# A two-layer graph attention: one program instead of six blocks, no global centre, first units on a quarter of the adjacency, layer 1 prepared in layer 0's last chunk

## The reference

```
# layer 0: 4 heads of width 32
Wh = (x @ W).reshape(N, 4, 32)
e  = leaky_relu(s_src[:, None, :] + s_dst[None, :, :], 0.2)      # s = <Wh, a>
att = softmax(where(adj > 0, e, -9e15), axis=1)
x  = layernorm(x + elu(att @ Wh))
# layer 1: one head of width 128, in a hyperbolic space
t  = logmap0(x)
e  = leaky_relu(t @ a[:128] + (t @ a[128:]).T, 0.2)
att = softmax(where(adj > 0, e, -9e15), axis=1)
out = layernorm(x + proj(expmap0(att @ t)))
```

## Time and profile before

| | us |
|---|---|
| median of 3 runs | 1024.91 (1024.4 to 1026.4) |
| the profiled execution | 1024.66 |
| its span, first to last instruction | 1022.8 |
| TensorE, VectorE, ScalarE busy in it | 867.5, 853.7, 584.0 |
| GpSimd busy | 55.9 |
| mean granted clock of TensorE | 0.932 of full speed |
| moved by DMA | 68.84 MB, 67 GB/s over the span |

### The profile page before, as it was taken

The page is one execution under the profiler, slowest core; times in us unless marked ns, Lnnn a source line. Parts: engine busy times, 40 slices in busy tenths (PEclk is TensorE's granted clock), DMA queues, the critical chain, the costliest instruction groups (busy, mean ns, idle before and its releaser), DMA issues. The chain is left out here.

```text
span 1022.8 us, 25271 instructions
## 1 busy us (share of the span) xinstructions
PE 867.5 (85%) x10996; PEld 712.4 (70%) x10996; DVE 853.7 (83%) x1576; ACT 584.0 (57%) x640; POOL 55.9 (5%) x59
## 2 busy tenths in 40 slices
PE   6714999998999989998899704598999999999990
PEld 5614999998999989998899704354555555555550
DVE  5797788899998999889999678989878878788716
ACT  2478889996999869998768114361332514315101
POOL 1231000000000000000000005200000000000000
PEclk9756999999999999999999956799999999999996
DMA  8937756632666327031000023002032020320000
GB/s 146 166 66 195 96 65 72 81 162 43 74 74 123 127 24 85 23 130 79 23 3 3 1 85 104 1 1 93 11 104 77 27 92 10 103 76 27 0 10 12
DMA packets 30187, 68.84 MB, mean 67 GB/s; under 512 B 1346, under 2 KB 22276, under 8 KB 29444
## 3 DMA queue, kind: packets, MB, share of 16 engines
q0 software_dynamic: 4608, 16.78, 17.1%
q1 hardware_dynamic: 23300, 48.47, 13.3%
q10 hardware_dynamic: 2176, 2.10, 0.6%
HBM read 96.54 MB, written 21.14 MB: 115 GB/s over the span
## 5 line engine op out<-in xcount | busy, mean ns | idle before, releaser
L857 PE MATMUL bank<-moving,ring 128*128 128x99 bf16 (+1 forms) x6400 | 453.4, 219 | 11.6 <-DVE ring L817 11.6
L857 PEld LDWEIGHTS bank<-moving,ring 128*128 128x128 fp8e4 x6400 | 386.3, 97 | 14.2 <-DVE ring L817 13.9
L773 ACT ACTIVATE ring<-s_rows,scores 128x1024 fp8e4<-128x1024 f32 x352 | 373.1, 1140 | 28.7 <-PE bank L857 19.0
L1317 PE MATMUL bank<-moving,pair 128*128 128x387 bf16 x1792 | 300.1, 329 | 3.4 <-DVE evac L1406 3.4
L1317 PEld LDWEIGHTS bank<-moving,pair 128*128 128x128 fp8e4 x1792 | 175.8, 98 | 127.8 <-DVE evac L1406 3.8
L857 PE MATMUL bank<-moving,masks 128*128 128x99 bf16 x1792 | 237.8, 208 | 30.2 <-DVE ring L807 20.6
L857 PEld LDWEIGHTS bank<-moving,masks 128*128 128x128 fp8e4 x1792 | 174.4, 98 | 32.0 <-DVE ring L807 20.8
L1243 ACT ACTIVATE small<-small 128x4 f32<-128x4 f32 x24 | 4.9, 206 | 219.3 <-DVE small L1189 180.5
L807 DVE SCALAR_TENSOR_TENSOR ring<-ring,masks 128x1024 int32<-128x1024 int32 x88 | 107.3, 1220 | 15.3 <-ACT ring L773 15.1
L788 DVE TENSOR_SCALAR ring<-s_rows,neg_d 128x1024 uint8<-128x1024 f32 x160 | 109.6, 750 | 1.7 <-PEq L910 1.6
L817 DVE TENSOR_TENSOR ring<-masks,ring 128x1024 int32<-128x1024 int32 x72 | 88.2, 1225 | 17.1 <-PE bank L857 15.0
(11 more groups left out here) (217 smaller groups left out, 581.1 us busy)
## 6 DMA issues: line engine op xcount, KB each, us to landing
adj_tiles<-in_adj_dram POOLq DMA_DIRECT2D x32, 512.0 KB, 8.3
masks_kept<-masks SPq DMA_DIRECT2D x4, 4096.0 KB, 14.8
pair<-masks_kept SPq DMA_DIRECT2D x8, 2048.0 KB, 8.7
s_rows<-score_rows SPq DMA_DIRECT2D x16, 512.0 KB, 3.9
feat<-in_x_dram SPq DMA_DIRECT2D x4, 512.0 KB, 5.5
values_kept<-masks SPq DMA_DIRECT2D x1, 2048.0 KB, 15.6
s_rows<-score_rows SPq DMA_DIRECT2D x8, 256.0 KB, 8.5
out_dram<-result ACTq DMA_DIRECT2D x8, 256.0 KB, 2.1
```

The source lines that it names most:

```text
L773: last = act.activation(j_tile(below, k), s_rows[:, h % 2, :], ACT.Sign, bias=scores[:, j, h:h + 1], saturate=False)
L857: last = pe.matmul(bank[b][:, at + lo:at + hi], mask, moving[:, j, h, lo:hi], start=first, stop=(j == T - 1), skip_group_check=True)
L1317: last = pe.matmul(bank[2 * t + side][:, 0:PARTS * K1], j_tile1(pair[:, y, side, :], j)[:, t * P:(t + 1) * P], moving1[:, j, side * PARTS ...
```

## The change

All of both layers' fast path is one block; general attention is a second block behind it. Its parts:

- `bounds` and `exponents` are gone, with the extrema, the centre, the mean of the values and the treatment of rows without neighbours. Exponentials are taken straight from the scores by ScalarE; the row factor is one `lift` in layer 0. One flag is raised late in layer 1 (`raise_flag`) from the scores' extrema, the variances, empty rows, and a check of the adjacency: 64 parts of 2048 integers per partition, each loaded by POOL (1 MB) into one of two buffers and put through a Square with accumulation on ScalarE (`check_part`), two or three behind each group of signs of runs 2 to 7.
- The adjacency of chunk 0 comes in four quarters of columns (`load_quarter`, `turn_quarter`, `take_quarter`), and a unit waits only for its quarter. Head 0's weights are split before the units, those of heads 1 to 3 beside units 0 to 6. The score rows of heads 0 and 1 come from four matmuls of 512 columns instead of through HBM.
- `DIRECT` marks 12 of 32 units; the transposes for chunk 1 begin at unit 12.
- `take_head` and `take_run` lose the steps for empty rows, and `finish_ask` its minimum.
- In the last chunk, VectorE and ScalarE do root, logarithm, gains and exponentials of the first three chunks' rows and the weights of group 0; the last chunk's rows follow in run 0, before group 3.
- All eight signs of a group of run 0 are ScalarE's; POOL splits no weights.
- Results are stored by SP, not by ScalarE. The product of the residual with the inverse deviation moves under the tanh. Runs are unrolled.

```diff
-    DIRECT = [how == "D" for how in H // 2 * ("DD-D----" "DD-D-D--")]
+    DIRECT = [how == "D" for how in H * "DD-D----"]
+    CHECKS = 64
+    CHECK = N * N // P // CHECKS
...
+        def load_quarter(pool, k):
+            for q in range(NB):
+                pool.dma_start(quarter[:, k % 2, :].rearrange("p (q r n) -> p q r n", r=2, n=C)[:, q, :, :],
+                               adj_blocks[:, q, :, k * C:(k + 1) * C]).then_inc(quarter_in[k % 2], 16)
...
+        def check_part(act, k):
+
+            act.wait_ge(check_loaded[k % 2], 16 * (k // 2 + 1))
+            if k >= 2:
+                act.wait_ge(check_done, k - 1)
+            act.activation(check_out[k % 2], check_in[k % 2], ACT.Square, bias=minus_one[:, 0:1], scale=2.0,
+                           accum_out=checks[:, k:k + 1], saturate=False).then_inc(check_done, 1)
...
+                pool.wait_ge(unit_done, NC * U)
+                for k in range(CHECKS):
+                    if k >= 2:
+                        pool.wait_ge(check_done, k - 1)
+                    pool.dma_start(check_in[k % 2], adj_flat[:, k * CHECK:(k + 1) * CHECK]).then_inc(check_loaded[k % 2], 16)
...
+                take_quarter(act, 0)
+                round_part(act, 0, 1)
+
+                for c in range(NC):
+                    for u in range(U):
+                        act_unit(act, c, u)
...
+                        if c == 0:
+                            if u in (1, 3, 5):
+                                round_part(act, u // 2 + 1, 0)
+                            if u in (2, 4, 6):
+                                round_part(act, u // 2, 1)
+                                if u == 4:
+                                    act.wait_ge(scores_out, 16)
+                                take_quarter(act, u // 2)
...
+                for e in range(NR):
+                    fast_closing.act(act, e)
+                    for g in range(NG):
+                        if e + 2 < NR:
+                            signs(act, e + 2, g)
+                        while done < min(CHECKS, CHECKS * (e * NG + g + 1) // (NG * (NR - 2))):
+                            check_part(act, done)
+                            done += 1
...
+                        if c == 0:
+                            if u in (0, 2, 4):
+                                weigh_values(dve, u // 2 + 1)
+                                take_high(dve, u // 2 + 1)
+                            if u in (1, 3, 5):
+                                take_middle(dve, u // 2 + 1)
...
+                        if c == NC - 1:
+                            if u == 15:
+                                roots_ask(step, rows, 0, EARLY, roots_asked)
+                            if u == 17:
+                                dve.wait_ge(roots_given, 1)
+                                logs_ask(step, rows, inv_std, 0, EARLY, logs_asked)
+                            if u == 19:
+                                dve.wait_ge(logs_given, 1)
+                                gains(step, rows, inv_std, 0, EARLY, d1, s1, scores1_ready)
+                            if u == 22:
+                                late_weights(0)
+                            if u == 23:
+                                dve.wait_ge(kept, 16 * (NC - 1))
+                                dve.wait_ge(unit_done, (NC - 1) * U)
+                                weigh_group(dve, 0)
...
+                for e in range(NR):
+                    take_run(step, e)
+                    if e + 2 < NR:
                         for g in range(NG):
+                            split_group(dve, e + 2, g)
+                    if e == NR - 2:
+                        raise_flag(step)
```

More of the change, by code:

```diff
@@ new lines, in wait_s, with act_unit @@
+        def wait_s(engine, c, u):
+            h = u // UH
+            if c == 0 and h < 2:
+                engine.wait_ge(s_first, 2 * (h + 1))
+            else:
+                engine.wait_ge(s_in[h % 2], c * 32 + 16 * (h // 2))
+        def act_unit(act, c, u):
+            h, g = divmod(u, UH)
+            if g == 0:
+                wait_s(act, c, u)
+            if not ON_ACT[u]:
+                return
+            wait_slot(act, c, u)
+            below = below_slot(c, u)
+            for k in range(JU):
+                last = act.activation(j_tile(below, k), s_rows[:, h % 2, :], ACT.Sign,
+                                      bias=scores[:, g * JU + k, h:h + 1], saturate=False)
+            last.then_inc(signs_ready, 1)
+            if g == UH - 1:
+                act.wait_ge(signs_ready, c * NA + act_count(u + 1))
+                act.sem_inc(s_read_act, 1)
@@ new lines, in pe_unit @@
+        def pe_unit(pe, c, u):
+            h, g = divmod(u, UH)
+            if c == 0 and g == 0:
+                pe.wait_ge(side_done, 2 * (h + 1))
+            pe.wait_ge(unit_ready, c * U + (u + 1))
+            below = below_slot(c, u)
+            for t in range(CT):
+                b, at = t // 2, (t % 2) * W0
+                if g == 0 and t % 2 == 0 and (c > 0 or h > 0):
+                    pe.wait_ge(acc_taken, c * (H * NB) + ((h - 1) * NB + b + 1))
+                for k in range(JU):
+                    j = g * JU + k
+                    mine = slice(t * P, (t + 1) * P)
+                    of_below = j_tile(below, k)[:, mine]
+                    if DIRECT[u]:
+                        of_all = j_tile(masks[:, c % 2, :], j)[:, mine]
+                        weighed = ((of_all, 0, PARTS * K0), (of_below, 0, W0))
+                    else:
+                        weighed = ((j_tile(above_slot(c, u), k)[:, mine], 0, PARTS * K0), (of_below, PARTS * K0, W0))
+                    for mask, lo, hi in weighed:
+                        first = j == 0 and t % 2 == 0 and mask is weighed[0][0]
+                        last = pe.matmul(bank[b][:, at + lo:at + hi], mask, moving[:, j, h, lo:hi],
+                                         start=first, stop=(j == T - 1), skip_group_check=True)
+                if g == UH - 1 and t % 2 == 1:
+                    last.then_inc(acc_ready, 1)
+                elif t == CT - 1:
+                    last.then_inc(unit_done, 1)
+            if g == UH - 1:
+                pe.wait_ge(acc_ready, c * (H * NB) + (h + 1) * NB)
+                pe.sem_inc(unit_done, 1)
@@ new lines, in _ @@
+                split_group(dve, 0, 0)
+                take_head(step, NC - 1, H - 1)
+                dve.wait_ge(unit_done, NC * U)
+                weigh_group(dve, 1)
+                take_high1(dve, 1)
+                take_middle1(dve, 1)
+                split_group(dve, 0, 1)
+                close_piece(NC - 1, 0)
+                weigh_group(dve, 2)
+                take_high1(dve, 2)
+                take_middle1(dve, 2)
+                split_group(dve, 0, 2)
+                for n in range(1, 5):
+                    close_piece(NC - 1, n)
@@ new lines, in two_layer_gat, with flagged @@
+        general0 = General(0, H, D, lambda it, h: one(scores[:, bass.ds(it, 1), H + h:H + h + 1]))
+        general1 = General(1, 1, F, lambda it, h: g_s1[:, bass.ds(it, 1)])
+        general_closing = Closing("g_close", work=g_work1, result=g_result, small=g_small, stats=g_stats,
+                                  mean_var=g_mean_var[:, 0:RT, :], inv_std=g_inv_std)
+        def flagged(engine):
+            return engine.If(engine.value_load(flag[0:1, 0:1], min_val=0, max_val=1) > 0)
+        with nc.Block() as block:
```

1918 lines of the change are left out of this document (899 added, 1019 removed).

## The result

The changed kernel takes 1035.7 us in the median of five runs (1033.0 to 1036.5), the kernel before beside it on the same chip 1024.9 (1023.2 to 1028.3). The ratio is 1.0096, with a 95% interval of 1.0072 to 1.012: about 1% slower. The forecast was 1028 us, the range 984 to 1052, and slower the likelier sign by little (0.47 against 0.44).

A forecast was written before the change was run, and what follows sets the result against it. TensorE and VectorE were near their limit in layer 0, TensorE never idle in layer 1; check loads would then bind layer 1's loops. Chunk 3's end 559.5 + 443.9 + tail 22.3 = 1025.7 us span, so 1028 us; range 984 to 1052.

The forecast's parts named there:

- First unit: Preparation before layer 0's attention: unit 0 starts at 45 us against 89.5, and chunk 0 ends 20.5 us sooner, at 191.
- Chunks 1 and 2: Layer 0's middle chunks: two fewer direct units each, TensorE 116.2 us plus 5 us of waits gives 121, -3.7 each.
- Chunk 3: Layer 0's last chunk: gains 15.3 us of layer 1's early preparation on VectorE, so 126.5 us against 120.7, +5.8.
- 127, less a lead of 6, then 5 us of TensorE behind it: Chunk 3's length: VectorE's 111.7 plus 15.3 us of added preparation, adjusted for lead and TensorE, put at 126.5 us.
- Between the layers: From chunk 3's end, VectorE's chain of weights, masks and closing pieces takes 79.8 us; TensorE's next run starts at 81, against 116.4.
- Layer 1: Check loads make each loop 53.35 us against TensorE's 42.9; from chunk 3's end 443.9 us against 416.6, +27.3.
- L + 2.0: A check buffer's cycle in layer 1: L, a 1 MB load's time to land (5.7 us), plus a 2.0 us check.
- Last run and tail: Layer 1's end: run 7 needs 42.9 us on TensorE; closing is 2.2 us shorter, so the tail falls from 24.5 to 22.3.
- A: Rival on layer 1's check loads: they land in 4.9 us, loop 50.95, 1013 us; faster from below 5.4. Chance 0.26.
- B: Rival on layer 1: loads don't limit, ScalarE's own 26.0 us stand, loop 44.75, 976 us. Chance 0.14.
- C: Rival on layer 1: loads slowed by mask loads and each other, landing in 6.6 us, loop 57.5, 1053 us. Chance 0.18.
- D: Rival on chunk 0: checks harmless but early start empty, chunk ends at 205; with A's loads 1027 us. Chance 0.04.

The follow-up runs named there:

- the run with the old pattern: Changed kernel with the kernel before's direct units (14 of 32 in a chunk, where the changed kernel has 12): 1041.3 us, ratio 1.016 to the kernel before.
- run 7: Not a follow-up experiment: the last of layer 1's runs inside the kernel, a stretch of TensorE matmuls, forecast at 42.9 us.
- the four kernels without that limit: Changed kernel without checks, 975.4 us; each buffer loaded once, 984.6; loads but no checks, 974.7; five half-size buffers with checks where ScalarE idles, 978.0.
- two of the experiments on layer 0: Apparently, each against the changed kernel: chunk 3's factors asked for three units sooner, 1041.4 us; the kernel before's pattern of direct units, 1041.3 us.

## Why the prediction came out as it did

The profiled execution's span was forecast at 1025.7 us and is 1033.8, 8.1 more. Step by step:

- **First unit.** Forecast 45 us, measured 40.0. Unit 2 began at 56.2 and unit 4 at 72.1, forecast 61 and 78, and the last mask of unit 6 was written at 86.9, forecast 93 and inside the 85 to 100 that the prediction allowed. The chunk followed: head 3 moved by -24.5, forecast -20.5. The account of the queues was right in kind (24.5 us are left of a head start of 49.5; the rest was hidden work made visible) and 4 us too careful.
- **Chunks 1 and 2.** Forecast -3.7 each, measured -0.5. The step that failed is "keeping the waits at 5 us". TensorE's time without work was 5.9 us in the middle chunk of before (124.8 less 118.9), not 5, and it grew to 7.2. Its busy time fell by 1.8 us (forecast 2.7) and VectorE's by 4.7. There are two buffers for the sides above, and an XOR waits until TensorE has read the older one. VectorE waited 11.5 us in chunk 2 for that alone (L579; 2.4 in the kernel before), TensorE 4.4 for VectorE. So a sum of one engine's work plus a constant wait didn't hold where two engines, busy for 94% and 90%, wait for each other. That this is the whole cause is read from the waits; the run with the old pattern leaves it open.
- **Chunk 3.** Forecast +5.8, measured +13.8. The step that failed is "127, less a lead of 6, then 5 us of TensorE behind it" (which is 126.0; the forecast says 126.5). It gives VectorE's own work next to no waits. VectorE's work came out smaller, 122.2 us between the marks of the table, but the engine also stood idle for 12.9, of which it waited 10.6 for TensorE to free one of the two buffers (L579). Without the preparation it waited there as well (8.5 us), so the added work had no idle time to hide in: it was sized at 15.3 us and costs 16.0, as the run that takes it out shows. Together these two steps cost 14.4 us, against 4 gained in chunk 0: layer 0's last matmul ended at 569.5, forecast 559.5, +10.0 (the rest is that head 3's reduction, the mark of the table, begins a little ahead of that end).
- **Between the layers.** Forecast 83.7 from the end of chunk 3 to the first run's closing (79.8 and 3.9 of reductions), measured 80.2: -3.5. The forecast had counted the chain on VectorE group by group; no run takes it apart.
- **Layer 1.** Forecast loops of 53.35 us, measured 53.1: -1.4 over six. The mechanism, the queue order, the pairs of checks with a wait in front, the place where TensorE idles: all are in the trace as described. Two of its terms missed and cancelled, which is luck. A load lands in 5.2 to 5.3 us, not 5.7; and a round has 0.4 us of hand-over that I left out: 5.3 + 2.0 + 0.4 = 7.7 is the L + 2.0 of the sum. The check took 2.00 us, forecast 2.0.
- **Last run and tail.** From the seventh closing to the end 65.4 us, forecast 62.4. After 8.7 us without work TensorE started run 7 at the lower clock:

```profile
965.60:970.60 5.00, 4.94 (x16) 2.37 (x17) 4.90 (x9) 1.83 (x3) 0.00 (x0) 0.50 0.57 208
971.00:1011.00 40.00, 39.85 (x240) 23.18 (x237) 16.71 (x70) 4.36 (x7) 0.00 (x0) 1.00 0.02 7
```

  A granted clock of 0.50 for 5 us, then 1.00: its first 16 matmuls took 5.24 us where a later 16 take 2.82. That is 2.4 of the 3.0; the sum had no such term. In the six loops before it the low clock cost nothing: between 649.7 and 1011.9 us VectorE waited for TensorE's banks only in the last run.

The sum's 8.1 us are thus a balance of larger errors of both signs. And the range, 984 to 1052, held every outcome from 4% faster to 3% slower, so that the time lay in it says little; what the runs bear out is the mechanism of layer 1.

**The rivals.** A (short loads) was half right: the loads did land under 5.4 us, from where it said faster, and the time was slower, since the hand-over made up for it. B named the time of a kernel whose loads don't limit, 976 us; the four kernels without that limit took 975 to 985. Its own case, checks without the wait for loads, took 984.6, since layer 0 ended later than forecast. C had the right sign and a wrong reason: the mask loads did collide (13.1 us to land, 8.7 before), but the run with loads alone had them land in 15.8 us at up to 386 GB/s, where the changed kernel had 247, and lost nothing. D didn't occur; the flag didn't rise.

The page's rule that I weighed against my L (the Trainium skill, DMA: Bandwidth & Descriptors, "Anatomy of one DMA": 2.0 us plus bytes over 436e3) gives 4.4 us for 1 MB and 3.2 for 512 KB. Here they took 5.2 to 5.3 and 4.0. The step between them, 1.2 to 1.3 us for 512 KB, is just the page's rate; its fixed part is 2.8 here and not 2.0. My own way, halving part of a 2 MB load that casts, missed by 0.4 on the other side.

## What to carry to other kernels

Before a stream of loads is added beside a full pipeline, count its round: landing, use, and hand-over, divided by the buffers, against the time between two uses. Sixty-four MB and 128 us of ScalarE were nearly free here; two buffers made them cost 60 us, half-size loads in two buffers 175, five half-size buffers with the uses placed in idle time 3 (each against 975). And ask of every inserted instruction who stands behind it in its queue: signs, closings and the flag each took their turn. Work that is moved forward into a stage costs its whole length if it goes to the engine that binds there; what it buys may be a DMA's trip that nobody had on the list.

## What the runs showed of the hardware

A wait of TensorE of 1.7 us at the same place of the same code is followed by a full clock in one trace and half a clock in another. First the changed kernel, then the kernel without checks, both just behind that wait in chunk 1 (window, busy us and count of each engine, clock, DMA share, GB/s):

```profile
220.40:223.70 3.30, 3.30 (x54) 3.30 (x52) 3.16 (x9) 3.24 (x4) 0.00 (x0) 1.00 0.87 88
```
```profile
220.40:223.70 3.30, 3.26 (x27) 3.09 (x28) 3.16 (x9) 3.30 (x4) 0.00 (x0) 0.51 0.93 88
```

In 3.3 us there are 54 matmuls at 2.4 GHz or 27 at 1.2 GHz. It costs 1.6 us each time, so 124.3 and 125.9 both occur for the same chunk: of the eleven traces with this code in chunk 1, the seven with a clock of 1.00 from 220 to 224 us took 124.2 to 124.3 us for it, the four with 0.57 to 0.70 took 125.9. Such losses are part of the scatter between runs of one kernel (3 to 9 us here); that they are all of it is not shown. They are why two of the experiments on layer 0 are read from their chunks and not from their totals.

ScalarE's check of 2048 integers with accumulation took 2.00 us, one of 1024 took 1.14. Behind each the trace shows a read of the accumulator of 0.19 us, but the next check starts on time, 1.99 us after the one before (770.67, 772.66): it costs nothing. With two 1 MB loads in flight and the mask loads beside them, the core's traffic reached 386 GB/s in one fortieth of the span.
